# One GpSimd queue, 32 gathers: the new key/value rows of a sequence issued in the half tile of its old rows

## The chip, the cores and the metric

The kernel runs on one core of one Trainium2 chip. The metric is device time in microseconds (us). TensorE (PE in the profile), VectorE (DVE), ScalarE (ACT), GpSimd (POOL) and SyncE (SP) each run their own instruction list in order and meet at semaphores; PEld is TensorE's weight load.

## What is computed

`x` is 32 sequences of 64 tokens with 512 features. Four layers follow each other, each added to its input. Cut to what matters here:

```python
# layer 0: attention over a paged key/value cache, window of 256 tokens
q, k = rope(rms(x @ Wq)), rope(rms(x @ Wk));  v = x @ Wv
k_blocks = k_blocks.at[blk, :, off, :].set(k)      # the sequence's 64 new rows ...
v_blocks = v_blocks.at[blk, :, off, :].set(v)
k_all, v_all = k_blocks[block_tables], v_blocks[block_tables]   # ... are read back with the old ones
p = softmax(where(allowed, q @ k_all.T / 16, -inf));  x = x + (p @ v_all) @ Wo
x = x + x @ w1[subject]                             # layer 1
x = x + base(x) + lora2(x)                          # layer 2: W_base and four folded adapters
x = x + x @ W3 + lora3(x)                           # layer 3
```

Block tables, cache lengths, subject and adapter indices are inputs, so the rows of each sequence are found at run time.

## The kernel before

Two sequences make one tile of 128 tokens; there are 16 tiles, and the main loop of every engine runs over k = 0..31, one **half tile** (one sequence) at a time. The order on each engine is written out by hand. Even k = 2t and odd k = 2t + 1 carry different parts of the work around them, so that the pattern repeats every two half tiles (a **pair**).

A sequence's window is 336 rows of keys and values (21 blocks of 16, 512 f32 each). It is gathered into one of four buffers `kv_s[b % 4]` (all four are parts of the tensor `windows`) by GpSimd: `gather(b, 0)` issues three indirect DMAs (line L455) that read the **old rows** from the cache (`kvrows_dram`), and `gather(b, 1)` three more that read the **new rows** from `newkv`, the scratch table that the kernel filled earlier. Each of the two leaves out the rows that belong to the other. Because both write the same buffer, `gather(b, 1)` first waits on `kv_in[b % 4]` until the old rows of b have landed. Both then count on that semaphore, and TensorE's `keys_t(b)` waits for all six.

Besides the gathers GpSimd computes `root("q", ...)`: `ms` to the power -0.5 into `rstd`, for the queries' norm (L428). It waits for `q_ms`, which VectorE signals in `query_sums` (L799); VectorE's `query_last` (L807) waits for the root, and TensorE's `queries_t` (L987) for `query_last`.

What sets the order around the change:

- GpSimd waits for `pv_mm >= k`, that is for the end of TensorE's `values(k - 1)` (L1104), before it gathers the old rows of sequence k + 3 into the buffer that `values(k - 1)` read last.
- TensorE at even k: `keys_t(k + 1)` (transposes of the gathered keys, L1073), `queries(t + 1)` (L959 on `wq`), `probs_t`, `scores`, `project` (L959 on `wo`), `values(k)`. At odd k: `keys_t(k + 1)`, `queries_t(t + 1)`, `probs_t`, `mix` (L1119), `scores`, `base` (L959 on `wf`), `ranks` (L1132), `values(k)`, `up(t - 1)` (L1138).
- `queries` writes the PSUM bank `gb` that `up` wrote just before, so it waits for `xo_ready`: ScalarE's `out_ev` (L597, destination shown as `w_late`) must have copied `gb` away.
- VectorE at even k: `attn_low`, `query_first`, `query_sums`, four `soft`, half of the scaling, `query_last`, `residual`, the other half of the scaling.

Of the kernel before, what the change touches and what calls it, by code (L numbers as in the profile page):

```python
# [7 lines left out]
NB, NT, D = 32, 64, 512  # L8
# [67 lines left out]
def build(nc, xt, xtok, kvrows, wkv, wq, wo, qs, ks, w1, wbn, wt, a2t, b2t, wpt, s2, w3, a3t, b3t, s3,  # L76
# [4 lines left out]
    with ctx:  # L81
# [17 lines left out]
        def con(name, rows=128):  # L99
            k, c, w = CONST[name]  # L100
            return cst[k][0:rows, c:c + w]
# [157 lines left out]
        def tables(eng, w):  # L259
            lo, hi = (nscale[w][:, 32 * a:32 * a + 32].unsqueeze(1).to_broadcast([128, TILES, 32]) for a in (0, 1))  # L260
            return [eng.tensor_tensor(costab[w][:, :, 0:32], cosx[:], lo, ALU.mult),
                    eng.tensor_tensor(costab[w][:, :, 32:64], cosx[:], hi, ALU.mult),
                    eng.tensor_tensor(sintab[w][:, :, 32:64], sinx[:], lo, ALU.mult),
                    eng.tensor_tensor(sintab[w][:, :, 0:32], nsinx[:], hi, ALU.mult)]
# [138 lines left out]
        @block.gpsimd  # L403
        def _(pool):
            P = nc.gpsimd
            P.memset(half[:], -0.5)
            P.memset(qt_s[1][:], 0.0)
            for i in range(2):
                P.memset(w1i[i][:], 0.0)
            P.memset(psum_p[0][:], 0.0).then_inc(S["zeroed"], 1)  # L410
            pool.wait_ge(S["zeroed"], 1)
            P.dma_start(newkv[0:1, :], qt_s[1][127:128]).then_inc(S["row0_stored"], 16)

            pool.wait_ge(S["slot_ready"], 1)
            for i in range(2):
                P.indirect_dma_start(blk_i[i][:], None, table, bass.IndirectOffsetOnAxis(ap=slots[:, i:i + 1], axis=0),
                                     bounds_check=NB * NSLOT + 3, oob_is_err=False).then_inc(S["l_table"], 16)
            pool.wait_ge(S["l_table"], 32)
            P.tensor_copy(blk[:, 0:WS], blk_i[0][:])
            P.tensor_copy(blk[:, WS:WX], blk_i[1][:, 0:NW]).then_inc(S["blk_ready"], 1)  # L420
            pool.wait_ge(S["blk_ready"], 1)
            pool.wait_ge(S["l_const"], 16)
            P.tensor_tensor(blkd.rearrange("p (s b) -> p s b", b=NB), blk[:].unsqueeze(2).to_broadcast([NB, WX, NB]),
                            con("ident", NB)[:, 0:NB].unsqueeze(1).to_broadcast([NB, WX, NB]), ALU.mult).then_inc(S["blkd_ready"], 1)

            def root(w, value, i):
                pool.wait_ge(S[w + "_ms"], value)
                P.tensor_tensor(rstd[i][:], ms[:], half[:], ALU.pow).then_inc(S[w + "_rstd"], 1)  # L428

            def split_low(k):  # L430
                pool.wait_ge(S["split_hi"], k + 1)
                P.tensor_tensor(splits[k][1], stage[k % STAGES][:], splits[k][0].bitcast(f32), ALU.subtract).then_inc(S["split_lo"], 1)

            split_low(0)
            split_low(1)
            root("k", 1, 0)
            pool.wait_ge(S["blkrow_ev"], 2)
            P.tensor_scalar(same[:, NW - 1, :], blkrow, blk[:, WX - 1:WX], None, ALU.is_equal).then_inc(S["same_ready"], 1)
            root("k", 2, 0)
            split_low(2)  # L440
            root("k", 3, 0)
            pool.wait_ge(S["scale_ready"], 1)
            pool.wait_ge(S["sin_done"], 1)
            q_tables = tables(P, "q")
            q_tables[-1].then_inc(S["qtab_ready"], 1)
            root("k", 4, 0)
            split_low(3)
            root("k", 5, 0)
            root("k", 6, 0)

            def gather(b, new):
                if new:
                    pool.wait_ge(kv_in[b % 4], 96 * (b // 4) + 48)
                for c in range(CH):
                    P.indirect_dma_start(  # L455
                        kv_s[b % 4][:, c, :], None, newkv if new else kvrows,
                        bass.IndirectOffsetOnAxis(ap=idx_all[:, new * CH + c, b:b + 1], axis=0),
                        bounds_check=NB * NT if new else NPOOL * BLOCK - 1, oob_is_err=False,
                    ).then_inc(kv_in[b % 4], 16)

            pool.wait_ge(S["idx_ready"], 16 * SP_)
            gather(0, 0)
            root("k", 7, 0)
            gather(1, 0)
            root("k", 8, 0)
            gather(2, 0)
            root("q", 1, 1)
            pool.wait_ge(S["row0_stored"], 16)
            for i in range(2):
                pool.wait_ge(kv_stored[i], 32 * (PAIRS // 2))  # L470
            gather(0, 1)
            gather(1, 1)
            gather(2, 1)
            gather(3, 0)
            gather(3, 1)
            root("q", 2, 1)

            for k in range(NB):
                if k >= 1 and k + 3 < NB:
                    pool.wait_ge(S["pv_mm"], k)  # L480
                    gather(k + 3, 0)
                if k >= 2 and k + 2 < NB:
                    gather(k + 2, 1)
                if k % 2 == 0 and 0 < k // 2 < TILES - 1:
                    root("q", k // 2 + 2, 1)


        @block.scalar
# [759 lines left out]
```

## Time and profile before

| what | value |
|---|---|
| time, median of 3 runs | 468.02 us (467.8 to 468.11) |
| the profiled execution: its own time | 468.45 us |
| its span, first to last instruction | 466.5 us |
| granted TensorE clock, mean | 0.989 |
| PE busy | 443.6 us, 95% of the span |
| DVE, ACT, POOL busy | 275.9, 226.5, 254.6 us |
| main loop, one pair (two sequences) | 21.84 us |

The span leaves out 1.95 us of the profiled execution's time. Busy time on PE counts pipelined matmuls with modelled ends, so it is no measure of how near the engine is to its peak; the waits tell more.

### The profile page before, as it was taken

What the parts mean: (1) busy time and instruction counts of PE and PEld (TensorE: products, weight loads), DVE (VectorE), ACT (ScalarE), POOL (GpSimd) and SP (SyncE); (2) the same over time, 40 slices, a digit from 0 to 9 for tenths busy, and PEclk for the clock granted to TensorE, in tenths of its full rate; (3) what the DMA queues carried; (4) which work ended last, traced back from release to release, by engine and by line L of the source; (5) the groups of instructions that cost most, each with busy time, mean ns of one, the idle gap of its engine ahead of it and who ended that gap; (6) DMA issues with size and microseconds to landing.
All of it is one profiled execution on the core that took longest, in us unless ns stands there. A gap on an engine that the chain in (4) does not pass through costs nothing.

```text
span 466.5 us, 9707 instructions
## 1 busy us (share of the span) xinstructions
PE 443.6 (95%) x2803; PEld 315.5 (68%) x2803; DVE 275.9 (59%) x801; ACT 226.5 (49%) x601; POOL 254.6 (55%) x240
## 2 busy tenths in 40 slices
PE   4989997999799999999999999999999999999985
PEld 2334444746587777787878777777778787878764
DVE  3997796465564747475656566464747465656410
ACT  1321223333754656473746565564656473746611
POOL 3368167834556666666565656666666666571000
PEclk9989999899999999999999999999999999999998
DMA  7649977764445554637364545555554646452220
GB/s 228 224 153 304 305 228 223 183 192 141 114 119 123 177 145 133 161 112 185 88 176 117 156 110 156 132 159 139 157 145 129 155 121 157 104 153 66 70 69 22
DMA packets 81402, 70.34 MB, mean 151 GB/s; under 512 B 51684, under 2 KB 57700, under 8 KB 81350
## 3 DMA queue, kind: packets, MB, share of 16 engines
q1 hardware_dynamic: 64688, 47.23, 36.1%
q0 software_dynamic: 15456, 22.08, 16.8%
q10 hardware_dynamic: 1206, 0.42, 0.5%
q8 instruction: 23, 0.38, 0.3%
q14 instruction: 29, 0.24, 0.2%
HBM read 79.66 MB, written 11.93 MB: 196 GB/s over the span
## 4 chain that ended last, share of the span: by engine, by line
PE 83%; DMA 4%; issue 4%; ACT 3%; POOL 3%; DVE 2%; POOLq 0%; SPq 0%; DVEq 0%
PE bank L959 27%; PE bank L972 13%; PE bank L1104 8%; PE bank L1092 8%; PE bank L1086 8%; PE bank L953 5%; DMA windows<-newkv,idx_all 3%; POOL windows L455 3%; PE bank L1138 3%; PE bank L1073 3%; PE bank L1119 2%; PE bank L1132 2%; ACT w_late L597 1%; DMA wkv_s<-wkv_dram 1%; PE bank L987 1%
## 5 line engine op out<-in xcount | busy, mean ns | idle before, releaser
L455 POOL DMA_INDIRECT windows<-kvrows_dram,idx_all x96 | 97.6, 1017 | 94.4 <-PE bank L1104 74.0
L455 POOL DMA_INDIRECT windows<-newkv,idx_all x96 | 95.9, 999 | 38.3 <-issue 28.9
L569 ACT ACTIVATE prob<-prob,negmax 128x336 f32<-128x336 f32 x128 | 72.5, 571 | 54.9 <-DVE negmax L859 54.9
L972 PE MATMUL bank<-wkv_s,xt_s 128*128 128x512 f32 x128 | 59.2, 623 | 8.2 <-DMA wkv_s<-wkv_dram 6.2
L859 DVE CUSTOM_DVE_ANT_0 prob<-bank,mask 128x336 f32<-128x336 f32 x128 | 57.1, 502 | 3.5 <-PE bank L1086 2.0
L575 ACT ACTIVATE pt_s<-bank 112x384 f32<-112x384 f32 x128 | 55.0, 484 | 2.4 <-PE bank L1092 2.4
L428 POOL TENSOR_TENSOR rstd<-ms,half 128x8 f32<-128x8 f32 x24 | 41.1, 1714 | 23.4 <-DVE ms L725 20.9
L1092 PE MATMUL bank<-cst,prob 128*112 128x128 f32 x384 | 53.9, 277 | 0.0
L1092 PEld LDWEIGHTS bank<-cst,prob 128*112 128x112 f32 x384 | 42.0, 133 | 17.1 <-issue 14.9
L972 PEld LDWEIGHTS bank<-wkv_s,xt_s 128*128 128x128 f32 x128 | 25.1, 200 | 40.1 <-issue 39.0
L1104 PE MATMUL bank<-pt_s,windows 112*64 112x128 f32 x768 | 49.4, 277 | 0.3 <-ACT pt_s L575 0.3
L792 DVE TENSOR_TENSOR t<-bank,qcos 128x512 f32<-128x512 f32 x16 | 11.1, 692 | 61.6 <-ACT sq L551 61.6
L869 DVE TENSOR_SCALAR prob<-prob,rinv 128x336 f32<-128x336 f32 x128 | 45.6, 398 | 2.3
L1104 PEld LDWEIGHTS bank<-pt_s,windows 112*64 112x64 f32 x768 | 41.2, 137 | 7.7 <-issue 5.8
L1086 PE MATMUL bank<-kt_s,qt_s 64*128 64x336 f32 x256 | 44.8, 468 | 0.3 <-issue 0.2
L959 PE MATMUL bank<-wq_hi,xq_hi 128*128 128x512 f32 x64 | 26.7, 417 | 3.9 <-DVE xq_lo L826 2.2
L1086 PEld LDWEIGHTS bank<-kt_s,qt_s 64*128 64x128 f32 x256 | 22.1, 186 | 11.5 <-issue 3.8
L959 PE MATMUL bank<-wf_hi,x_hi 128*128 128x512 f32 x64 | 27.3, 426 | 2.2 <-DVE x_lo L826 2.2
L563 ACT ACTIVATE kt_s<-bank 128x336 f32<-128x336 f32 x64 | 25.3, 449 | 8.2 <-PE bank L1073 7.9
L551 ACT ACTIVATE sq<-bank 128x512 f32<-128x512 f32 x16 | 9.6, 597 | 39.9 <-PE bank L959 39.9
L1073 PEld LDWEIGHTS bank<-cst,windows 112*128 112x128 f32 x192 | 19.4, 140 | 12.4 <-DMA windows<-newkv,idx_all 8.3
L959 PE MATMUL bank<-wo_hi,ot_hi 128*128 128x512 f32 x64 | 26.7, 417 | 0.8 <-ACT w_late L597 0.8
(174 smaller groups left out, 768.2 us busy)
## 6 DMA issues: line engine op xcount, KB each, us to landing
xt_s<-xt_dram SPq DMA_DIRECT2D x32, 256.0 KB, 4.3
mask<-masks_dram SPq DMA_DIRECT2D x32, 168.0 KB
newkv<-kvo SPq DMA_DIRECT2D x16, 256.0 KB, 4.0
stage<-xtok_dram SPq DMA_DIRECT2D x16, 256.0 KB
tsel<-ttab SPq DMA_DIRECT2D x64, 64.0 KB
out_dram<-w_late SPq DMA_DIRECT2D x16, 256.0 KB, 4.2
stage<-utab SPq DMA_DIRECT2D x32, 64.0 KB
wbn_late<-utab SPq DMA_DIRECT2D x32, 64.0 KB
```

Source lines behind the costliest of these rows:

```text
L428: P.tensor_tensor(rstd[i][:], ms[:], half[:], ALU.pow).then_inc(S[w + "_rstd"], 1)
L455: P.indirect_dma_start(kv_s[b % 4][:, c, :], None, newkv if new else kvrows, bass.IndirectOffsetOnAxis(ap=idx_all[:, new * CH + c, b:b + 1 ...
L569: A.activation(pr, pr, ACT.Exp, bias=negmax[:, g:g + 1], scale=-1.0, accum_out=psum_p[b % 2][:, g:g + 1]).then_inc(S["exp_done"], 1)
L575: A.activation(pt_s[g][:], tb[g % 2][0:KP, 0:CH * 128].rearrange("p (c q) -> p c q", c=CH), ACT.Copy).then_inc(S["pt_ev"], 1)
L859: V.tensor_tensor_reduce(out=prob[b % 3][:, g, :], in0=sbk[g][:, 0:WK], in1=mask[b % 3][:], scale=-1.0 / 16, scalar=3.0e38, op0=ALU.add, o ...
L869: V.tensor_scalar(pr, pr, rinv[b % 2][:, g:g + 1], None, ALU.mult).then_inc(S["norm_done"], 1)
L959: last = mm(to, lhs(a, c), rhs(b, c), start=(c == 0 and a == b), stop=(c == C - 1 and a == 1 and not more))
L972: last = mm(to[:], xt_s[n % 4][:, c, :], wkv_s[:, c, :], start=(c == 0), stop=(c == C - 1))
L1073: last = nc.tensor.transpose(sbk[p][:, KP * c:KP * c + KP], kv_s[b % 4][:, c, 128 * p:128 * p + 128], ident[0:KP, 0:KP])
L1086: mm(sbk[g][:, 0:WK], qt_s[t % 2][r, cols], kt_s[b % 2][p][r, :], start=True, stop=True).then_inc(S["s_mm"], 1)
L1092: last = nc.tensor.transpose(tb[g % 2][0:KP, 128 * c:128 * c + 128], prob[b % 3][:, g, KP * c:KP * c + KP], ident)
L1104: last = mm(ob[64 * h:64 * h + 64, col:col + 128], kv_s[b % 4][:, c, 256 + 64 * g:320 + 64 * g], pt_s[g][:, c, :], start=(c == 0), stop=(c ...
```

## The change

In the half tile k, the new rows that are issued are no longer those of sequence k + 2 (whose old rows were issued one half tile before) but those of sequence k + 3, whose old rows are issued in this same half tile. The queries' root, which stood behind both gathers, now stands between them.

```diff
@@ gpsimd, main loop
                 if k >= 1 and k + 3 < NB:
                     pool.wait_ge(S["pv_mm"], k)
                     gather(k + 3, 0)
-                if k >= 2 and k + 2 < NB:
-                    gather(k + 2, 1)
                 if k % 2 == 0 and 0 < k // 2 < TILES - 1:
                     root("q", k // 2 + 2, 1)
+                if k >= 1 and k + 3 < NB:
+                    gather(k + 3, 1)
```

The instruction lists of the four other engines are the same in both kernels. On GpSimd, at the head of the main loop (k = 1, 2, 3 and the old rows of k = 4), the list before reads as follows; `kvrows_dram` marks old rows, `newkv` new ones, `rstd1` the queries' root.

```order
L455 DMA windows<-kvrows_dram,idx_all 112x512 x6
L455 DMA windows<-newkv,idx_all 112x512 x3
L428 TENSOR_TENSOR rstd1<-ms,half 128x8
L455 DMA windows<-kvrows_dram,idx_all 112x512 x3
L455 DMA windows<-newkv,idx_all 112x512 x3
L455 DMA windows<-kvrows_dram,idx_all 112x512 x3
```

The first row is six old-row DMAs in a row: three for sequence 4 at k = 1 and three for sequence 5 at k = 2. The same place in the changed kernel:

```order
L455 DMA windows<-kvrows_dram,idx_all 112x512 x3
L455 DMA windows<-newkv,idx_all 112x512 x3
L455 DMA windows<-kvrows_dram,idx_all 112x512 x3
L428 TENSOR_TENSOR rstd1<-ms,half 128x8
L455 DMA windows<-newkv,idx_all 112x512 x3
L455 DMA windows<-kvrows_dram,idx_all 112x512 x3
L455 DMA windows<-newkv,idx_all 112x512 x3
L455 DMA windows<-kvrows_dram,idx_all 112x512 x3
```

Each old triple is now followed by the new triple of the same sequence, and at even k the root has moved ahead of the new triple. From there on the pattern repeats: the piece of the difference for one pair of half tiles on GpSimd in the middle of the program is

```order
 L455 DMA windows<-kvrows_dram,idx_all 112x512 x3
 L455 DMA windows<-newkv,idx_all 112x512 x3
 L455 DMA windows<-kvrows_dram,idx_all 112x512 x3
+L428 TENSOR_TENSOR rstd1<-ms,half 128x8
 L455 DMA windows<-newkv,idx_all 112x512 x3
-L428 TENSOR_TENSOR rstd1<-ms,half 128x8
```

Here only the root changes its row; that the two `newkv` triples belong to one sequence later than before, and so wait for other landings, the rows' names don't show.

## Rows read from the trace of the kernel before

**Rows 1.** The page: busy time by engine, chain that ended last, GpSimd's DMA queue.
```profile
PE 443.6 (95%) x2803; PEld 315.5 (68%) x2803; DVE 275.9 (59%) x801; ACT 226.5 (49%) x601; POOL 254.6 (55%) x240
PE 83%; DMA 4%; issue 4%; ACT 3%; POOL 3%; DVE 2%; POOLq 0%; SPq 0%; DVEq 0%
q0 software_dynamic: 15456, 22.08, 16.8%
```

**Rows 2.** Waits, whole span: engine line <- releaser: us in total, times, longest.
```profile
POOL windows L455 <- PE bank L1104: 74.0, 28, 4.7
POOL windows L455 <- DMA windows<-kvrows_dram,idx_all: 9.5, 1, 9.5
PEld bank L1073 <- DMA windows<-newkv,idx_all: 8.3, 13, 1.0
```

**Rows 3.** Timeline of PE, three pairs: start, us, engine line op [idle <-releaser].
```profile
234.10 1.12 PE L1138 MATMUL bank<-stage,w_late 128*128 128x512 f32 x2
...
236.00 0.47 PE L959 MATMUL bank<-wq_hi,xq_hi 128*128 128x512 f32 x1 [0.20 <-ACT w_late L597]
...
255.94 1.12 PE L1138 MATMUL bank<-wbn_late,w_late 128*128 128x512 f32 x2
257.26 0.79 PE L1073 MATMUL bank<-cst,windows 112*128 112x112 f32 x6 [0.20 <-DMA windows<-newkv,idx_all]
257.84 0.47 PE L959 MATMUL bank<-wq_hi,xq_hi 128*128 128x512 f32 x1
...
267.84 0.79 PE L1073 MATMUL bank<-cst,windows 112*128 112x112 f32 x6
...
277.78 1.12 PE L1138 MATMUL bank<-stage,w_late 128*128 128x512 f32 x2
...
279.69 0.47 PE L959 MATMUL bank<-wq_hi,xq_hi 128*128 128x512 f32 x1 [0.20 <-ACT w_late L597]
```

**Rows 4.** Timeline of PEld at two even half tiles.
```profile
234.96 0.63 PEld L1073 LDWEIGHTS bank<-cst,windows 112*128 112x128 f32 x6 [0.57 <-DMA windows<-newkv,idx_all]
...
257.25 0.59 PEld L1073 LDWEIGHTS bank<-cst,windows 112*128 112x128 f32 x6 [1.02 <-DMA windows<-newkv,idx_all]
```

**Rows 5.** Timeline of ACT between those two TensorE rows.
```profile
257.10 0.60 ACT L597 ACTIVATE w_late<-bank 128x512 f32<-128x512 f32 x1 [0.45 <-PE bank L1138]
```

**Rows 6.** Timeline of POOL: sequence 2's last old issue, the loop's head, one pair.
```profile
78.18 0.98 POOL L455 DMA_INDIRECT windows<-kvrows_dram,idx_all  x1 [0.30 <-issue]
...
112.17 2.04 POOL L428 TENSOR_TENSOR rstd<-ms,half 128x8 f32<-128x8 f32 x1 [0.21 <-DVE ms L799]
118.90 1.06 POOL L455 DMA_INDIRECT windows<-kvrows_dram,idx_all  x1 [4.69 <-PE bank L1104]
...
132.71 2.05 POOL L428 TENSOR_TENSOR rstd<-ms,half 128x8 f32<-128x8 f32 x1 [0.55 <-DVE ms L799]
...
256.83 0.98 POOL L455 DMA_INDIRECT windows<-kvrows_dram,idx_all  x1 [2.41 <-PE bank L1104]
...
260.71 0.99 POOL L455 DMA_INDIRECT windows<-newkv,idx_all  x1 [0.30 <-issue]
...
264.30 1.68 POOL L428 TENSOR_TENSOR rstd<-ms,half 128x8 f32<-128x8 f32 x1
268.74 1.05 POOL L455 DMA_INDIRECT windows<-kvrows_dram,idx_all  x1 [2.76 <-PE bank L1104]
```

**Rows 7.** Timeline of DVE: `query_last` at k = 2; sums and `query_last` of the pair.
```profile
136.50 0.68 DVE L807 TENSOR_TENSOR qrot<-t,rstd 128x512 f32<-128x512 f32 x1
...
263.49 0.17 DVE L799 TENSOR_SCALAR ms<-ss 128x8 f32<-128x8 f32 x1
...
267.55 0.68 DVE L807 TENSOR_TENSOR qrot<-t,rstd 128x512 f32<-128x512 f32 x1
```

**Rows 8.** The chain, 244 to 262 us: one new-row DMA from its issue to its landing.
```profile
253.43 3.78 DMA windows<-newkv,idx_all
```

**Rows 9.** GpSimd's DMA queue from 81 to 82 us: packets, MB, share.
```profile
q0 software_dynamic: 2, 0.00, 0.6%
```

## The prediction

> **What bounds the kernel now.** I read the page first: TensorE is busy for 95% of the span and holds 83% of the chain that ended last; DMA and POOL together hold 7% of it [rows 1]. The question is whether that 7%, the gathers, is a loss that an earlier issue gives back. The list of waits seems to say so: TensorE's weight loads for `keys_t` waited 13 times for new rows, 8.3 us in all, 1.0 us at most [rows 2].
>
> The timeline of TensorE says otherwise. At an even half tile it does `up` (L1138), `keys_t` (L1073), `queries` (L959 on `wq`). In the pair at 236 us `keys_t` waited 0.57 us for the DMA, in the pair at 258 us 1.02 us [rows 4]. Yet from the start of `up` to the start of `queries` it is 236.00 - 234.10 = 1.90 us, 257.84 - 255.94 = 1.90 and 279.69 - 277.78 = 1.91 [rows 3]. The late landing changes nothing, since `queries` can't start earlier: it needs the bank `gb`, which `out_ev` on ScalarE empties from 257.10 to 257.70 [rows 5], and in the two pairs where the rows came earlier `queries` shows just that wait, 0.20 us for `w_late` L597 [rows 3]. `keys_t` fits into the hole that `out_ev` leaves. The pairs agree: from `up` to `up` it is 21.84 us, both times [rows 3]. The chain went through POOL and DMA in the pair at 258 only because two paths of nearly equal length end there.
>
> GpSimd is no bound either: it waited 28 times for `values`, 74.0 us in all [rows 2], 2.4 to 2.8 us per half tile in the steady state [rows 6].
>
> **The change part by part.**
>
> *New rows one half tile earlier.* The 96 new-row DMAs are the same in number and size; the POOL rows show 1.29 us from one issue to the next, (260.71 - 256.83) / 3 [rows 6]. What this removes is TensorE's wait for new rows. Its value is what `queries` gains: 0 in the pair with the 1.02 us wait by the comparison above. At odd half tiles `keys_t` shows no such wait (the row at 267.84) [rows 3]. Worth 0.0 us; its cover is `out_ev`, and without that cover it would be up to 8.3 us.
>
> *The wait for old rows.* `gather(b, 1)` waits for the landing of `gather(b, 0)`. Before, a half tile lay between the two and the wait ended at once: it shows once only, 9.5 us [rows 2], ahead of the main loop for sequence 3, where old and new rows stood side by side already, behind nine other new-row DMAs. Now GpSimd stands still for it in each of the 28 half tiles. How long, no steady row shows. From below: after the last old issue of sequence 2, which ended at 79.16 [rows 6], the queue still had two packets after 81 us [rows 9], so at least 1.8 us. A new triple in the steady state landed 3.78 us after the start of its last issue [rows 8], 2.8 us after the issue's end. From above: 9.5 us. I take L = 2.8 us, as that row is of the same queue beside the same traffic; the 9.5 us are from a stretch with twelve of these DMAs in a row. The Trainium skill ("DMA: Bandwidth & Descriptors", Anatomy of one DMA) gives 2.0 us plus bytes over 436 GB/s; with 22.08 MB over 192 gathers [rows 1], 0.115 MB each, that is an estimate of 2.3 us, and no row here isolates its two terms. By it the sum below would be 0.5 us shorter.
>
> *GpSimd's new round.* I follow one pair, starting at `ms`, which ends at 263.66 [rows 7]. GpSimd is already there, waiting, if the round fits.
> - Wake-up 0.2 and root 2.04: a root that was waiting for `ms` took that in the row at 112.17 [rows 6]; in a queue it took 1.68. The root ends at 265.9, against 265.98 before. Old rows of this half tile, issued before it, land meanwhile (if L is under about 3.9), so that wait is free at even k.
> - 0.2 and new triple 3.57 (three of 0.99 and two gaps of 0.30): 269.7.
> - Odd half tile: `values` is done (GpSimd was released at 268.74 before), so no wait for it any more; gap 0.3, old triple 3.57: 273.6. L = 2.8: 276.4. 0.2 and new triple: 280.1.
> - Next even half tile: gap and old triple 3.87: 284.0. The next `ms` is at 263.66 + 21.84 = 285.5.
>
> The sum is 20.3 us of 21.84: GpSimd arrives 1.5 us before `ms`, and is set back by it in every pair, so nothing adds up. GpSimd's odd old triples go out 1.2 us later than before (269.9 against 268.74), the even ones too.
>
> *What is late next.* Behind the waiting gather stand, at odd k, the new triple and the next old triple, then the root; who waits for them: `keys_t` on TensorE and `query_last` on VectorE. New rows: sequence 18's leave at 280.1 and land at about 283, and `keys_t(18)` comes at 267.84 + 21.84 = 289.7, so 6.7 us to spare; sequence 17's leave at 269.7, land at 272.5, and `keys_t(17)` comes a pair after 257.26, at 279: over 6 us [rows 3]. The root: ready at 265.9, `query_last` starts at 267.55 [rows 7]: 1.65 us to spare. All costs are covered: 0.0 us.
>
> *The head of the loop.* At k = 1 GpSimd now waits for sequence 4's old rows too. Their issue starts at 118.90 and takes until 122.5 as before [rows 6]; with L they have landed at 125.3, the new triple takes until 129.1, sequence 5's old triple until 133.0, and the root starts at 133.0 instead of 132.71, where it waited for `ms` itself [rows 6]. VectorE takes it at 136.50 [rows 7], 1.5 us after its end. Also covered. From there the round above takes hold.
>
> *The tail.* The last gather now goes at k = 28 instead of k = 29; TensorE has no wait for it.
>
> **Sum.** 0.0 (waits of TensorE that hid behind `out_ev`) + 0.0 (28 waits of GpSimd in its own idle time). On the profiled execution: 468.45, of which the span is 466.5 and 1.95 lies around it; that execution is 0.43 above the median, so I forecast the median, **468.0 us**.
>
> **The rivals.**
>
> *A, the forecast:* nothing on TensorE's path moves. For it: three equal distances despite unequal DMA waits. **0.80.**
>
> *B, the landing was the bound:* if `queries` does start earlier, the 13 waits come back, 468.0 - 8.3 = 459.7. For it: the chain's row through `newkv` [rows 8]. Against it: the pair with 1.02 us of wait is no longer than the one with 0.57. **0.07**, with smaller shares of it.
>
> *C, the landing wait becomes GpSimd's bound (slower):* its place is the odd half tile. It decides when L passes 2.8 + 1.5 (spare before `ms`) + 1.65 (spare before `query_last`) = 5.95 us at every odd k. Each us beyond costs one us in each of the 14 pairs, as VectorE's `query_last` is late, then `queries_t`. At L = 6.5 that is 0.55 x 14 = 7.7: 475.7 us; at the upper bound 9.5 it would be 3.55 x 14 = 50: 518 us. For it: the row with 9.5, and that SP's transfers share the DMA engines. Against: the steady row, 2.8. The Trainium skill speaks for this rival ("DMA: Bandwidth & Descriptors", Rules for kernel authors): issue a DMA early, compute, wait for its semaphore late, since the fixed cost then overlaps. By that rule the old order was the right one for GpSimd; the trace shows neither order's cost until the room of 5.95 us is used up. Chance of C: **0.09.**
>
> *D, a single stall at the head (slower):* if sequence 4's old rows take 9.5 instead of 2.8 to land, as sequence 3's did, the root of k = 2 comes 6.7 + 0.3 later than before with 1.74 us to spare (134.76 to 136.50) [rows 6, 7]: +5.3, 473.3 us. Against: by then the DMAs ahead of it are gone. **0.04.**
>
> **How the numbers follow.** The three runs before lie within 0.3 us, so about 0.2% (0.9 us) is what can be told from no change. Case A's own range is 467.1 to 468.9. B falls on the faster side (0.07); C and D, 0.13, on the slower; I give slower a little of the range: 467.0 to 469.2, which leaves out under 2 in 10. Faster 0.07, within 0.2% 0.80, slower 0.13.
>
> **What would show it.** In the changed profile: `PEld L1073 <- newkv` gone from the waits (was 8.3 us); `up` to `queries` still 1.90 and `up` to `up` still 21.84; `POOL L455 <- PE L1104` down from 74.0 to under 15; a new row `POOL L455 <- kvrows_dram` of about 14 x 2.8 = 39 us beside the old 9.5, almost all at odd k; some 14 x 1.5 = 21 us more of `rstd L428 <- DVE ms`; POOL's busy time up by 12 x 0.36 = 4 us from roots that wake up. I am wrong if DVE's L807 waits for `rstd`, or if the pair shrinks with the vanished DMA waits.

## The result, and the profile after

The changed kernel takes 471.84 us (median of 12 runs, 470.47 to 474.17), the kernel before 469.06 us beside it (12 runs, 467.16 to 471.57). The ratio is 1.0068 with a 95% interval of 1.0045 to 1.009: slower by about 3.2 us (2.1 to 4.2). The forecast was 468.0 with a range up to 469.2, so it was wrong: rival C's mechanism came, though the landing stayed far below the 5.95 us that the forecast had set as its condition. Times in this document are medians of all executions, while ratios and intervals use only those in the faster of the two states of a kernel, so a ratio need not be the quotient of the two medians.

The page after, lines that answer to [rows 1]: the span, the busy times, the chain by engine.

```profile
span 472.2 us, 9707 instructions
PE 447.8 (95%) x2803; PEld 318.2 (67%) x2803; DVE 277.6 (59%) x801; ACT 226.8 (48%) x601; POOL 259.3 (55%) x240
PE 30%; DMA 20%; issue 20%; POOL 19%; DVE 7%; ACT 2%; POOLq 1%; ACTq 0%; DVEq 0%
```

TensorE held 83% of the chain, now 30%; DMA, issue and POOL hold 59%. The busy shares hardly moved and would not have told this.

The waits of the kernel after (us in total, times, longest), those that the forecast named:

```profile
POOL windows L455 <- DMA windows<-kvrows_dram,idx_all: 81.7, 28, 9.1
...
POOL windows L455 <- PE bank L1104: 4.7, 1, 4.7
POOL rstd L428 <- DVE ms L799: 4.5, 3, 1.9
DVE qrot L807 <- issue: 3.4, 6, 0.6
PEld bank L987 <- DVE qrot L807: 3.2, 6, 0.5
```

Beside [rows 2]: the wait for `values` fell from 74.0 to 4.7 us, and TensorE's row for `newkv` is gone. Both as forecast. The wait for old rows is 81.7 us, not some 48, and the last two rows are new: six times VectorE's `query_last` came late, and TensorE's `queries_t` (L987) behind it. For the first of the two the profile names no releaser (`issue`), so the root as its cause is read from the times. At one of the six, GpSimd's root and then `query_last`:

```profile
225.37 1.68 POOL L428 TENSOR_TENSOR rstd<-ms,half 128x8 f32<-128x8 f32 x1
...
227.15 0.69 DVE L807 TENSOR_TENSOR qrot<-t,rstd 128x512 f32<-128x512 f32 x1 [0.57 <-issue]
```

The root ends at 227.05 and `query_last` starts 0.10 us later.

TensorE's first and last pair of the loop, the middle ones of [rows 3], and one late `queries_t`:

```profile
148.83 0.70 PE L1138 MATMUL bank<-stage,w_late 128*128 128x512 f32 x1
...
214.89 1.13 PE L1138 MATMUL bank<-wbn_late,w_late 128*128 128x512 f32 x2
...
227.90 0.66 PE L987 MATMUL bank<-cst,qrot 128*128 128x128 f32 x4 [0.32 <-DVE qrot L807]
...
237.27 1.12 PE L1138 MATMUL bank<-stage,w_late 128*128 128x512 f32 x2
...
239.17 0.47 PE L959 MATMUL bank<-wq_hi,xq_hi 128*128 128x512 f32 x1 [0.20 <-ACT w_late L597]
...
436.32 1.12 PE L1138 MATMUL bank<-wbn_late,w_late 128*128 128x512 f32 x2
```

From `up` to `queries` it is 239.17 - 237.27 = 1.90 us, as before: this step held. But the pair is now 237.27 - 214.89 = 22.38 us in place of 21.84. Over 13 pairs it is 436.32 - 148.83 = 287.49 us. The same two rows of the kernel before:

```profile
146.74 0.70 PE L1138 MATMUL bank<-stage,w_late 128*128 128x512 f32 x1
...
430.66 0.70 PE L1138 MATMUL bank<-wbn_late,w_late 128*128 128x512 f32 x1
```

430.66 - 146.74 = 283.92, so the loop is 3.57 us longer, within the ratio's 2.1 to 4.2. Four pairs are still 21.84 or 21.83 us, six are 22.37 or 22.38, and three lie between, 21.94 to 21.99. The nine longer ones are those in which `query_last` starts 0.1 us behind the root's end and later after `ms` than before the change, and together they make up the 3.57 us. The profiled execution differs by more, 472.2 - 466.5 = 5.7 us; 148.83 - 146.74 = 2.1 of that is ahead of the loop. The granted clock there (windows: us, busy of the five engines, clock, DMA share, GB/s), first after, then before, then the kernel before in another run (e5 below):

```profile
126.00:132.00 6.00, 4.70 (x15) 3.69 (x16) 1.85 (x4) 0.93 (x4) 4.62 (x5) 0.72 0.67 176
```

```profile
126.00:132.00 6.00, 5.22 (x29) 3.84 (x30) 2.85 (x7) 1.67 (x4) 4.78 (x5) 1.00 0.91 227
```

```profile
126.00:132.00 6.00, 5.58 (x20) 4.28 (x22) 1.27 (x3) 0.93 (x3) 4.57 (x5) 0.72 0.89 232
```

0.72 is a mean: in the kernel after, the granted clock is 0.50 (1.2 GHz, the lower level) from 128 to 130 us, after TensorE was busy for only 0.18 of the 2 us from 125 to 127. It needs no change to come: the kernel before shows the same 0.72 in e5, where the first `up` starts at 147.97 us. In e5 to e8, in a group where the kernel before takes 469 us too, the first `up` starts anywhere from 144.35 to 147.97, and e6, with the change in it, at 147.11. The 148.83 of the run here lies 0.9 us above them all, and one execution can't tell what that is.

**GpSimd's round.** Its timeline after, one pair and the next stand; it answers to [rows 6].

```profile
239.29 0.99 POOL L455 DMA_INDIRECT windows<-newkv,idx_all  x1 [3.60 <-DMA windows<-kvrows_dram,idx_all]
...
245.77 0.99 POOL L455 DMA_INDIRECT windows<-kvrows_dram,idx_all  x1 [0.30 <-issue]
246.79 1.67 POOL L428 TENSOR_TENSOR rstd<-ms,half 128x8 f32<-128x8 f32 x1
250.45 1.14 POOL L455 DMA_INDIRECT windows<-newkv,idx_all  x1 [1.99 <-DMA windows<-kvrows_dram,idx_all]
...
257.09 0.99 POOL L455 DMA_INDIRECT windows<-kvrows_dram,idx_all  x1 [0.30 <-issue]
261.99 0.99 POOL L455 DMA_INDIRECT windows<-newkv,idx_all  x1 [3.91 <-DMA windows<-kvrows_dram,idx_all]
...
269.60 1.68 POOL L428 TENSOR_TENSOR rstd<-ms,half 128x8 f32<-128x8 f32 x1
272.58 1.05 POOL L455 DMA_INDIRECT windows<-newkv,idx_all  x1 [1.30 <-DMA windows<-kvrows_dram,idx_all]
...
283.89 0.99 POOL L455 DMA_INDIRECT windows<-newkv,idx_all  x1 [3.78 <-DMA windows<-kvrows_dram,idx_all]
```

The two rounds are 261.99 - 239.29 = 22.70 and 283.89 - 261.99 = 21.90 us, 22.3 in the mean, against a pair of 21.84. These two are longer than most: over the 11 rounds from 172.92 to 416.73 us, counted the same way, the mean is 22.16, beside the 287.49 / 13 = 22.11 of TensorE's pairs. GpSimd and TensorE thus go at one pace, a slower one than before. The root follows the old triple without a gap: GpSimd no longer waits for `ms`; `ms` has been ready for some time when GpSimd comes to the root. It stands twice per round: 3.6 to 3.9 us at odd k in these rows (3.6 to 4.1 in the loop from 172.92 us on) and 1.3 to 2.0 at even k behind the root (0.9 to 2.0). What the first of these stands consists of, by the chain (start, us, what):

```profile
257.09 4.12 DMA windows<-kvrows_dram,idx_all
261.21 0.02 issue
...
261.99 0.35 POOL windows L455
```

The last old issue ends at 258.08 and lands at 261.21, 3.13 us later. Then 261.99 - 261.21 = 0.78 us pass until the next issue runs.

### The profile page after: what moved, and what is told of

Same layout as the page of the kernel before. It is cut to its first block, busy times and chain, and to the rows that moved or that the text cites. A ratio compares the mean times of both kernels' runs of the same rounds, so it can differ in the third digit from the quotient of the medians.

```text
span 472.2 us, 9707 instructions
## 1 busy us (share of the span) xinstructions
PE 447.8 (95%) x2803; PEld 318.2 (67%) x2803; DVE 277.6 (59%) x801; ACT 226.8 (48%) x601; POOL 259.3 (55%) x240
## 4 chain that ended last, share of the span: by engine, by line
PE 30%; DMA 20%; issue 20%; POOL 19%; DVE 7%; ACT 2%; POOLq 1%; ACTq 0%; DVEq 0%
DMA windows<-kvrows_dram,idx_all 19%; POOL windows L455 18%; PE bank L959 7%; PE bank L972 7%; PE bank L953 5%; PE bank L1086 2%; DMA cst<-const_dram 2%; PE bank L1104 2%; PE bank L1092 2%; PE bank L1138 1%; ACT prob L569 1%; PE bank L1119 1%; PE bank L1030 1%; PE bank L1057 1%; PE bank L1132 1%
## 5 line engine op out<-in xcount | busy, mean ns | idle before, releaser
L455 POOL DMA_INDIRECT windows<-newkv,idx_all x96 | 97.8, 1018 | 102.2 <-DMA windows<-kvrows_dram,idx_all 81.7
L455 POOL DMA_INDIRECT windows<-kvrows_dram,idx_all x96 | 98.6, 1027 | 33.3 <-issue 28.6
L428 POOL TENSOR_TENSOR rstd<-ms,half 128x8 f32<-128x8 f32 x24 | 42.8, 1782 | 23.5 <-DVE ms L725 18.6
L1092 PEld LDWEIGHTS bank<-cst,prob 128*112 128x112 f32 x384 | 42.0, 133 | 17.0 <-issue 14.9
L792 DVE TENSOR_TENSOR t<-bank,qcos 128x512 f32<-128x512 f32 x16 | 11.1, 692 | 63.2 <-ACT sq L551 59.0
```

Of the source, the lines that this page charges most:

```text
L455: P.indirect_dma_start(kv_s[b % 4][:, c, :], None, newkv if new else kvrows, bass.IndirectOffsetOnAxis(ap=idx_all[:, new * CH + c, b:b + 1 ...
L1092: last = nc.tensor.transpose(tb[g % 2][0:KP, 128 * c:128 * c + 128], prob[b % 3][:, g, KP * c:KP * c + KP], ident)
```

## The experiments

There were 18 runs in five groups; runs of one group share a chip and the runs of the kernel before. **One thing is needed to read the table:** in four of the five groups the kernel before itself takes 530 to 543 us, only in the second (e5 to e8) 469, as when the result was measured. Only the second group speaks directly of the 3.2 us, and the changed kernel as it stands was not run in it; there its place is taken by the run of the result. e10, e11 and e12 are four executions each and are classed as unclear on record.

| run | edit | this, us | before, us | ratio, 95% |
|---|---|---|---|---|
| e1_after_again | the change | 537.35 | 539.8 | 0.9922 (0.9877 to 0.9966) |
| e2_root_only | root moved alone | 598.52 | 539.8 | 1.1078 (1.1024 to 1.1132) |
| e3_odd_late | no new rows at odd k | 510.99 | 539.8 | 0.946 (0.9413 to 0.9507) |
| e4_after_dve_root | root on VectorE | 516.63 | 539.8 | 0.9564 (0.9516 to 0.9612) |
| e5_before_again | kernel before, one execution | 470.36 | 469.44 | |
| e6_after_extra_behind | one operation more | 493.54 | 469.44 | 1.0534 (1.0476 to 1.0591) |
| e7_odd_late | as e3 | 467.71 | 469.44 | 0.9976 (0.9939 to 1.0013) |
| e8_after_dve_root | as e4 | 468.61 | 469.44 | 0.9996 (0.9961 to 1.0031) |
| e9_after_again | the change | 530.7 | 532.03 | 1.0012 (0.9954 to 1.007) |
| e10_root_only | as e2 | 589.86 | 532.03 | 1.1124 (1.106 to 1.1188) |
| e11_before_extra | before, one operation more | 529.53 | 532.03 | 0.9889 (0.9804 to 0.9974) |
| e12_after_extra_under | operation under the stand | 533.02 | 532.03 | 1.0067 (1.0004 to 1.0131) |
| e13_after_extra_under | as e12 | 531.47 | 531.81 | 0.9951 (0.9895 to 1.0007) |
| e14_before_extra | as e11 | 529.46 | 531.81 | 0.9945 (0.9898 to 0.9991) |
| e15_root_only | as e2 | 592.28 | 531.81 | 1.1144 (1.1056 to 1.1233) |
| e16_after_again | the change | 533.07 | 531.81 | 1.0011 (0.9959 to 1.0063) |
| e17_after_extra_under | as e12 | 536.5 | 543.22 | 0.9873 (0.9824 to 0.9922) |
| e18_before_extra | as e11 | 539.13 | 543.22 | 0.9962 (0.9911 to 1.0012) |

The theory after the result: GpSimd's round is longer than the pair, and this reaches TensorE by one way alone, the late root, `query_last`, `queries_t`. The expectations call it theory R. The rival, under several letters there: the gathers, sent out at other times, hold TensorE up by themselves, at `keys_t` or through traffic.

**One operation more in the round (e6).** The edit adds one operation of the root's kind at the end of odd half tiles; nobody reads its result.

```diff
                 if k >= 1 and k + 3 < NB:
                     gather(k + 3, 1)
+                if k % 2 == 1 and k < NB - 3:
+                    P.tensor_tensor(spare[:, 8 * (k // 2):8 * (k // 2) + 8], half[:], half[:], ALU.pow)
```

> The changed kernel with one more GpSimd operation of the root's kind (1.7 us, its result unused) behind the new rows of every odd half tile. Theory R: GpSimd's round is the bound, so every pair grows by the whole 1.7 us: 13 x 1.7 = 22 us over the changed kernel, about 494 us (on a slow chip as much in difference). Rival H or T (GpSimd's length is not the bound): under 4 us more.

It took 493.54 us. Timeline of GpSimd (lines have moved by one), one round; then VectorE's `query_last` behind that root; then the waits.

```profile
292.16 0.99 POOL L456 DMA_INDIRECT windows<-newkv,idx_all  x1 [3.85 <-DMA windows<-kvrows_dram,idx_all]
...
295.74 1.68 POOL L488 TENSOR_TENSOR spare<-half 128x8 f32<-128x8 f32 x1
297.61 1.05 POOL L456 DMA_INDIRECT windows<-kvrows_dram,idx_all  x1 [0.18 <-issue]
...
301.62 1.67 POOL L429 TENSOR_TENSOR rstd<-ms,half 128x8 f32<-128x8 f32 x1
```

```profile
303.38 0.69 DVE L810 TENSOR_TENSOR qrot<-t,rstd 128x512 f32<-128x512 f32 x1 [0.57 <-issue]
```

```profile
DVE qrot L810 <- issue: 15.4, 11, 2.0
PEld bank L990 <- DVE qrot L810: 15.2, 11, 2.1
```

The root ends at 303.29 and `query_last` starts at 303.38. Over the 13 pairs from 147.11 to 456.04 us (the starts of the first and the last `up`) a pair is 23.76 us, 1.65 more than the 287.49 / 13 = 22.11 of the kernel after, for an operation of 1.68. GpSimd is the bound of the loop, and in this run work outside its two stands costs one to one. The same operation in the kernel before, where GpSimd waits for TensorE, was never measured in a group of 469 us (see e11, e14 and e18), so that it would be free there is argued and not shown.

**One stand less (e7).** At odd k no new rows are issued. At even k GpSimd issues old rows, then both triples of new rows with the root between them.

```diff
                     gather(k + 3, 0)
+                if k >= 2 and k % 2 == 0 and k + 2 < NB:
+                    gather(k + 2, 1)
                 if k % 2 == 0 and 0 < k // 2 < TILES - 1:
                     root("q", k // 2 + 2, 1)
-                if k >= 1 and k + 3 < NB:
+                if k >= 1 and k % 2 == 0 and k + 3 < NB:
                     gather(k + 3, 1)
```

> The same kernel as e3, with the kernel before beside it. Theory R: one stand for a landing per round, GpSimd has 2 us or more of room, pairs of 21.84 and ratio 0.998 to 1.002. If the gain of 5% in e3 belongs to the order and not to the chip, the ratio is near 0.95 again.

467.71 us, ratio 0.9976; its interval lies below that of the change (1.0045 to 1.009) altogether. The waits, and GpSimd's timeline at an even half tile and at the start of the next even one:

```profile
POOL windows L455 <- PE bank L1106: 71.3, 15, 5.0
...
POOL windows L455 <- DMA windows<-kvrows_dram,idx_all: 8.0, 1, 8.0
```

```profile
285.93 1.68 POOL L428 TENSOR_TENSOR rstd<-ms,half 128x8 f32<-128x8 f32 x1
287.79 1.06 POOL L455 DMA_INDIRECT windows<-newkv,idx_all  x1 [0.18 <-issue]
...
300.30 0.98 POOL L455 DMA_INDIRECT windows<-kvrows_dram,idx_all  x1 [4.98 <-PE bank L1106]
```

With a triple and the root between an old triple and the wait for it, the wait costs nothing, the pairs are 21.82 us (one 21.87) and GpSimd waits 5 us for TensorE again. So the exposed stands are the loss: with none left open in the loop (the 8.0 us are ahead of it), the loop is as long as before. This version keeps the earlier issue for the sequences k + 3 of even k, half of all, and its time can't be told from the kernel before.

**The root off GpSimd (e8).** The round keeps both stands, but the queries' root is gone from GpSimd. In its place VectorE computes a reciprocal, so the queries are scaled by 1/`ms` and not by its root; the output differs in that.

```diff
 # gpsimd, main loop (and the two calls ahead of it)
-                if k % 2 == 0 and 0 < k // 2 < TILES - 1:
-                    root("q", k // 2 + 2, 1)
 # vector, query_sums, behind the operation that writes ms
+                dve.wait_ge(S["q_ms"], t + 1)
+                V.reciprocal(rstd[1][:], ms[:]).then_inc(S["q_rstd"], 1)
```

> The same kernel as e4 (root replaced by VectorE's reciprocal, so the queries are scaled by 1/ms). Theory R with the root as the only way to TensorE: pairs of 21.84 until GpSimd has fallen back by some 6 us, so ratio 0.998 to 1.003. Rival K (the gathers themselves hold TensorE up): 1.007 or more.

468.61 us, ratio 0.9996, again altogether below the change's interval. Waits, and GpSimd's stands in one round:

```profile
POOL windows L455 <- DMA windows<-kvrows_dram,idx_all: 103.1, 29, 7.0
...
PEld bank L1071 <- DMA windows<-newkv,idx_all: 0.2, 1, 0.2
```

```profile
388.98 0.99 POOL L455 DMA_INDIRECT windows<-newkv,idx_all  x1 [3.99 <-DMA windows<-kvrows_dram,idx_all]
...
410.72 0.98 POOL L455 DMA_INDIRECT windows<-newkv,idx_all  x1 [3.71 <-DMA windows<-kvrows_dram,idx_all]
```

GpSimd stands longer than in the change (103.1 us). Its round is 410.72 - 388.98 = 21.74 us in these rows, but 22.04 in the mean of the 12 rounds from 157.14 to 421.67 us, near the change's 22.16 and above TensorE's pair. Yet TensorE's `keys_t` waits once, 0.2 us. The rival falls: the gathers go out at the change's pace and hold nobody. The cost came through the root.

The pairs are not quite those of before: 21.90 to 22.11 us, 21.97 in the mean, 285.56 for the 13, 1.64 us more than 283.92. VectorE computes the reciprocal between `ms` and `query_last` here, whose starts are 4.25 us apart in place of 4.06, and `queries_t` waited for `query_last` four times, 1.1 us in all. So this edit has a small cost of its own, and the 1.64 us can't be charged to GpSimd by any row.

**The kernel before once more (e5)**, one execution, without an edit.

> One look at the kernel before on this chip, so that the other runs of the group have its trace beside them. In the group of the four runs before this one the kernel before took 540 us and the traces showed idle time on all engines that is put down to issue or to no releaser; if that was the chip, this run is back at 468 to 471 us with pairs of 21.84, if it was not, it is near 540 again.

Its list of waits has this row:

```profile
PEld bank L1073 <- DMA windows<-newkv,idx_all: 11.1, 14, 1.2
```

11.1 us of waits, more than the 8.3 of [rows 2], and most pairs are 21.82 us. e7 has one such wait and the same pairs: those waits were worth nothing, as forecast.

**The change where TensorE's pair is longer (e1, e9, e16).** No edit.

> The changed kernel once more, as the yardstick of this group. Theory R (the round): GpSimd's work for two half tiles, 12 issues at 1.30 us and two stands of 3.7 to 3.9 us for landings, one of them over the root, takes about 22.3 us, and TensorE's pair takes 21.84, so pairs of 22.38 appear and the time is 3 us above the kernel before. Rival H (the head): the surplus is a lower granted clock in the part ahead of the loop, which would go away in other runs; then the ratio here is within 0.2% of 1 and the pairs are 21.84.

> The changed kernel as yardstick of this group. Theory R: ratio 1.005 to 1.009, some half of the pairs at 22.4, the others at 21.84. If the group falls on a chip as slow as that of e1 to e4, this says nothing on R.

> The changed kernel as yardstick: ratio 1.004 to 1.010 on a chip of the usual speed.

Ratios 0.9922, 1.0012 and 1.0011: no loss there, and in e1 even a gain of 0.8%. The loss expected in each of the three did not come. From e1's waits (the second row names no engine of this core as the releaser):

```profile
POOL rstd L428 <- DVE ms L799: 53.6, 16, 5.1
...
ACT kt_s L563 <- remote: 41.8, 22, 3.2
```

In e1 the pairs take 22.98 to 31.43 us, for reasons that the trace doesn't show. GpSimd's round of some 22.2 us then fits, the root waits for `ms` 16 times where it did 3 times, and TensorE shows no wait for `query_last`. That agrees with the theory; what slows TensorE there stays open.

**The root moved alone (e2, e10, e15).** In the kernel before, the root goes ahead of the new rows of k + 2.

```diff
-                if k >= 2 and k + 2 < NB:
-                    gather(k + 2, 1)
                 if k % 2 == 0 and 0 < k // 2 < TILES - 1:
                     root("q", k // 2 + 2, 1)
+                if k >= 2 and k + 2 < NB:
+                    gather(k + 2, 1)
```

> The kernel before with the root alone moved between the two gathers; the new rows remain those of sequence k + 2, so no landing is waited for. Theory R: the round is 17.2 us of 21.84, the root comes 2 us earlier at most, nothing gains by it: ratio 1.000, pairs of 21.84. Rival P (the root's new place does the harm, beside VectorE's sums or by a late pv_mm): ratio near 1.007 as in the changed kernel.

> The kernel before with only the root moved between the gathers, now beside a normal yardstick. By the traces the root waits for ms until 6.8 us after the half tile's start and ends 2 us later, and the new rows of sequence k + 2, which TensorE needs at the start of the next half tile, stand behind it: they leave some 5 us later than before, so keys_t at odd k waits 3 to 4 us in each of 14 pairs. Expected 40 to 60 us slower, ratio 1.09 to 1.12. The first theory for this kernel (harmless, ratio 1.000) fell in e2, if that was not the chip.

> As e10. On a chip of the usual speed: new rows held behind the root by its wait for ms, 3 to 5 us of waiting in keys_t at odd k in each of 14 pairs, 40 to 70 us slower.

Ratios 1.1078, 1.1124 and 1.1144; in e2 I had taken it to be harmless, and that was wrong. GpSimd's timeline in e2, then TensorE's:

```profile
294.53 2.04 POOL L428 TENSOR_TENSOR rstd<-ms,half 128x8 f32<-128x8 f32 x1 [3.33 <-DVE ms L799]
296.76 1.06 POOL L455 DMA_INDIRECT windows<-newkv,idx_all  x1 [0.19 <-issue]
```

```profile
302.94 1.38 PE L1073 MATMUL bank<-cst,windows 112*128 112x112 f32 x6 [4.27 <-DMA windows<-newkv,idx_all]
```

The root waits 3.33 us for `ms`, the new rows stand behind it, and TensorE wants them at the start of the next half tile, where it waits 4.27 us. So of the change's two parts the move of the root alone is bad, and it takes the earlier issue (rows for k + 3 are needed a half tile later) to make it bearable. It is 58.7 us in e2, 4.2 in each of 14 pairs; the list of waits has 65.4 us in 15 times for `keys_t`. The mean granted clock was 0.91 as well, where the kernel before had 0.97 in that group, and the runs don't part the two. In a group where the kernel before takes 469 us this one wasn't tried.

**No new rows at odd k, and the root on VectorE, in the first group (e3, e4).** Edits as in e7 and e8.

> The changed kernel, but at odd k no new rows: those go at the next even k, ahead of the root, and only the new rows of the even half tile's own sequence are issued behind its old ones. One stand for a landing is left in a round instead of two, and the root and three more issues... lie over it. Theory R: the round is about 15.5 + 1.7 + at most 2 = 19 us, ratio 1.000, pairs of 21.84. Rival T (the early new rows collide with other transfers): about half of the surplus stays, ratio 1.003.

> The changed kernel with the queries' root taken off GpSimd: VectorE takes the reciprocal of ms instead, so the queries are scaled by 1/ms and not by its square root. GpSimd has only gathers in the loop. Theory R in its full form (the late root is the way by which GpSimd's round reaches TensorE): pairs stay 21.84 although GpSimd's round stays 22.3 to 22.8; GpSimd falls back some 0.7 us per pair, and has about 6 us to spare before keys_t, so at most the last pairs grow: ratio 0.998 to 1.003. Rival K (TensorE is held up by the gathers themselves): ratio 1.007 or more, as in the changed kernel.

0.946 and 0.9564 of the kernel before, where no difference was expected, and far more than the change's 0.8% there. e3's shortest pair is 23.26 us, so TensorE is slowed there too, only less. Why these two suffer less is not settled; neither gain is there in e7 and e8.

**The operation under the stand, and in the kernel before (e12, e13, e17; e11, e14, e18).** The operation of e6, once between the old and the new triple of the change, once at the end of the half tile of the kernel before.

```diff
                     root("q", k // 2 + 2, 1)
+                if k % 2 == 1 and k < NB - 3:
+                    P.tensor_tensor(spare[:, 8 * (k // 2):8 * (k // 2) + 8], half[:], half[:], ALU.pow)
                 if k >= 1 and k + 3 < NB:
                     gather(k + 3, 1)
```

> The changed kernel with the same extra operation, but between the old and the new rows of the odd half tile, under the wait for the landing. Theory R (the stand for the landing is what the round pays, not the work): the operation fits into the 3.8 us, and the time is that of the changed kernel within 0.3%, ratio 1.005 to 1.010. Rival W (any work adds to the round): 22 us more, as in e6.

> As e12: the changed kernel with the extra 1.7 us operation under the odd half tile's wait for the landing. On a chip of the usual speed, theory R: ratio to the kernel before 1.005 to 1.010, as the changed kernel. Rival W: 1.05, as e6, in which the same operation stands behind the new rows.

> As e13. If the chip is of the usual speed: theory R 1.005 to 1.010, rival W 1.05. If it is a slow one again, within 0.5% of the kernel before, which tells nothing between the two.

> The kernel before with the extra GpSimd operation of 1.7 us behind everything of each odd half tile, as in e6. Theory R: GpSimd idles 5.2 us per pair here, so nothing moves: ratio 0.998 to 1.003. Rival (any more work on GpSimd costs, whatever the round): 1.01 to 1.05.

> As e11. On a chip of the usual speed, theory R: GpSimd has 5.2 us of idle time per pair in the kernel before, ratio 0.997 to 1.003. Rival: over 1.01.

> As e14. If the chip is of the usual speed: theory R 0.997 to 1.003, rival over 1.01. On a slow one 0.990 to 1.000 as in e11 and e14.

All six lie between 0.987 and 1.007, but in these groups the change itself costs nothing, so the times don't tell the theories apart. GpSimd's timeline of e12 tells one thing:

```profile
304.31 0.99 POOL L456 DMA_INDIRECT windows<-kvrows_dram,idx_all  x1 [0.30 <-issue]
305.33 1.67 POOL L486 TENSOR_TENSOR spare<-half 128x8 f32<-128x8 f32 x1
308.43 1.05 POOL L456 DMA_INDIRECT windows<-newkv,idx_all  x1 [1.43 <-DMA windows<-kvrows_dram,idx_all]
```

From the old triple's end at 305.30 to the new triple it is 3.13 us with 1.67 us of work inside. In e9, the change in the same group, GpSimd stands mostly 2.9 to 3.2 us there with no work inside. So the stand has room for the operation. That e6's 493.54 us would fall to the change's time with the operation there wasn't seen, as no such run fell into a group of 469 us.

## Why the prediction was wrong

- **New rows earlier, 0.0 us: right.** `up` to `queries` is still 1.90 us, and the waits that vanished gave nothing back. Rival B is out.
- **The step that failed is "The sum is 20.3 us of 21.84".** By the rows after, against its terms: the stand at odd k is 3.91 and 3.78 us, not 2.8 + 0.2; the stand at even k is 1.99 and 1.30, not 0.2; the root is 1.7 with its gap, not 2.24; the twelve issues are 15.1, not 14.9. For the first round 20.32 + 0.91 + 1.79 - 0.54 + 0.22 = 22.70, for the second 20.32 + 0.78 + 1.10 - 0.53 + 0.23 = 21.90, as measured.
- **Landing, L = 2.8: nearly right.** It was 3.1 us after the issue's end at odd k (261.21 - 258.08) and 2.2 at the next even k. The upper end of 9.5 came only ahead of the loop (9.1 after).
- **The wake-up of 0.2 us was mis-sized.** It was taken from the root at 112.17, but the 0.21 there is how long GpSimd stood idle, not how long it took to wake up: that root starts 0.08 us after `ms` ends, and then takes 2.04 in place of 1.68 us. And a root is not a gather. A waiting gather takes 0.78 us from the landing to the start of its issue. The trace of before showed that already, where `gather` waited for `values`: the chain there, after the last matmul's end,

```profile
246.08 0.02 issue
...
246.90 0.37 POOL windows L455
```

  with 246.90 - 246.08 = 0.82 us.
- **"So that wait is free at even k" failed by its own premise.** It was free while GpSimd came 1.5 us before `ms` and the root took 2.04 on top. Each 0.1 us that the odd stand grew took cover from the even one, so the two stands are one sum: with no wait for `ms` the round is 15 + 2 (L + wake-up), whichever root lies under one of them. It passes 21.84 when L + wake-up passes 3.4 us. It was 3.8 in the mean at odd k and 3.35 at even k (1.7 under the root and 1.65 open), which gives 15.1 + 7.2 = 22.3 for the two rounds shown; the mean of the loop is 22.16.
- **Rival C's threshold of 5.95 us was wrong for that reason and for one more:** it added the 1.65 us between the root and `query_last` as if each pair had it anew. A round longer than the pair is late by more in every pair; such a spare is used up once. The rows show it: `query_last` was late by 0.57 us or so in six of the 13 pairs and by 0.1 to 0.2 in three more, a little at a time and never by much.
- **Its price, "one us in each pair": right.** 22.11 - 21.84 = 0.27 us in each of 13 pairs is the 3.57; e6 shows the same at 1.65 for 1.68.
- **What would show it:** `query_last` waiting is the sign that the text itself gave for being wrong, and `rstd <- ms` at 4.5 us, where some 21 more were to come, is a sign of being right that stayed away. GpSimd's busy time rose by 4.7 us, about as forecast, but more of it from slightly longer issues than from roots that wake up.
- **The head of the loop:** no stall, as forecast; D is out.

The Trainium skill's rule ("DMA: Bandwidth & Descriptors", Rules for kernel authors), to issue a DMA early, compute, and wait late, was cited for C. The traces agree with it now: with the wait right behind the issue it is open for 81.7 us, with a triple and the root between them (e7) for 8.0, once, ahead of the loop.

## What to carry to other kernels

An engine that only issues DMAs has a round time like any other: add up its issues and every wait that stands directly behind its own transfer, and compare with the loop of the engine that sets the pace; a spare downstream is used up once, not in each round. Take a wait's cost from a row of the same kind of waiting instruction, here 0.8 us for a gather and not what a root shows. If a transfer must wait for another of the same engine, put the engine's other work between the two.

## What was not expected of the hardware

The same program took 469 us in one group and 530 to 543 in four, with a mean granted clock of 0.96 to 0.98 where it was 0.99. The record has the chip's number 7 for the second group (469 us) and for the fifth (543 us) alike, so whether the chip makes the difference stays open; in the slower ones engines stand idle with no releaser on the core (`ACT kt_s` 41.8 us for "remote"). The ratios of one edit then differ: the change 1.0068 or 0.992 to 1.001, the version of e3 and e7 0.946 or 0.998. A waiting gather needs 0.78 us from the landing to its start, a waiting root 0.08 us (112.09 to 112.17).
